# Attention with a pair sum added by an accumulating transfer, and two sum rounds on TensorE instead of three

## The chip, the cores and the metric

The kernel runs on one core of one Trainium2 chip. The metric is the time of one execution on the device in microseconds (us). The kernel before takes 3239.81 us, the median of three runs (3238.47 to 3241.17). Engine names: PE is TensorE's matmul, PEld its weight load, DVE is VectorE, ACT is ScalarE, POOL is GpSimd, SP is SyncE, whose queue issues all transfers of the kernel before.

## What is computed

One transformer block in float32, for 8 batches of 1024 tokens with 512 features: x plus attention of the normalised x, then that plus a gated feed-forward part. The change touches the attention alone. Its core is this, with 16 heads of 32 features, so that a group of four heads fills 128 partitions:

```python
attn = jnp.einsum('bhqd,bhkd->bhqk', query, key) / scale
attn = jax.nn.softmax(attn, axis=-1)
out = jnp.einsum('bhqk,bhkd->bhqd', attn, value)
```

The kernel takes the exponentials first, multiplies them with the values, and divides by their sum over the keys later. The change is in how this sum over the keys is built.

## The kernel before, in words

Four stages follow each other: fold_block folds the weights, project_block makes queries, keys and values, attend_block does the attention, mix_block the output projection and the feed-forward part. attend_block goes through 32 groups (a batch and four heads, step(i, r, n)). A group has 8 units, four for each half of the queries (qc = 0 and 1, 512 queries each). I number halves through as h = 2n + qc. A unit is two tiles of 128 keys for each of four heads: 8 score tiles of 128x512.

For each unit TensorE computes 8 score tiles (L804) into three PSUM buffers, and between them 8 products of the next group (L264) from which VectorE takes row maxima (L280); at two places in a group (units 4 and 0) a transpose of the collected maxima (L259) stands between them and VectorE turns it into the row that SP then writes into the next group's queries (L277, L290). ScalarE takes the exponential of each score tile (L892) into one of three buffers probs, each a whole unit. After the scores of unit u TensorE multiplies the probabilities of unit u - 1 with the values (pv, L817). GpSimd adds the two key tiles of a unit (L911): one 128x2048 addition, the pair sum pairs[w], w = 0 to 3 for the unit in its half. After pair sum 1 it adds pair sum 0 onto it (L915). I call the sum of two pair sums a quad.

The sum over the keys is finished by TensorE in sums(n, qc): rounds of four matmuls with a matrix of ones (L828), each over one buffer of pairs, accumulated in PSUM; a float32 matmul shows as two records. There are three rounds, over pairs[1] (the quad), pairs[2] and pairs[3]. They stand after the scores and pv of unit 4 for the first half and of unit 0 of the next group for the second. ScalarE copies the result out (take_l, L876) before the exponentials of the unit that follows, just after the output of the half (take_o, L869), and SP stores both (L749, L754).

The order on each engine is written out by hand, with counting semaphores between engines. GpSimd waits before it writes pairs[w]: for w = 0 until its own quad of the half before is done, for the others until TensorE's round over the buffer in the half before is done. ScalarE waits, before it writes a probs buffer, for pv and for the pair sum of the unit three before it. L_AT says at which score tile the PSUM buffer of the sums is taken from the three. SP's queue, in order: the 10 loads for the group after next (L242 to L247), stores of the last half, the row of maxima, stores of the first half, the row of maxima of the second.

Of the kernel before, what the change touches and what calls it, by code (L numbers as in the profile page):

```python
# [21 lines left out]
ALU = mybir.AluOpType  # L22
# [20 lines left out]
def is_first(c):  # L43

    return type(c) is int and c == 0
# [161 lines left out]
NQ = S // CH  # L207
# [466 lines left out]
def attend_block(nc, sem, held, t, att, scratch, o_d, l_d):  # L674
# [5 lines left out]
    ROUNDS = KT // KB  # L680
    UNITS = NQ * ROUNDS
    UT = KB * HG
    TILES = UNITS * UT
    SR = 3
    PR = 3
    ADDED = [1, 2, 4, 5]
    ADDS = ROUNDS + 1
    SUMMED = [1, 2, 3]
    SUMS = len(SUMMED)
    RUN = TILES + NQ  # L690
    L_AT = UT
    HALF_RUN = ROUNDS * UT + 1
    assert RUN % SR == 0 and R3 * UNITS % PR == 0

    def is_last(n):
        return type(n) is int and n == NG - 1

    def place(e):

        return e + (e >= L_AT) + (e >= L_AT + ROUNDS * UT)  # L700

    def l_place(n, qc):

        return RUN if is_last(n) and qc == NQ - 1 else L_AT + (qc + 1) * HALF_RUN

    def taken(n, v):

        if is_first(n):
            return v + (v < L_AT)
        return n * RUN + v  # L710

    with ExitStack() as ctx:
        def sb(name, shape, dt=F32):
            return ctx.enter_context(nc.sbuf_tensor(name, shape, dt))
# [6 lines left out]
        pairs = sb("pairs", [P, ROUNDS, HG, CH])  # L721
# [8 lines left out]
        exped = sem("exped")  # L730
        pv_done = sem("pv_done")
        pair_done = sem("pair_done")
        sum_done = sem("sum_done")
        o_out = sem("o_out")
        o_stored = [sem(f"o_stored{q}") for q in range(NQ)]
# [3 lines left out]
        def rounds(step):  # L739

            for n in range(NG):
                step(n // R3, n % R3, n)
# [49 lines left out]
        @block.tensor  # L792
        def _(pe):
            def scores(n, r, u, x):
                qc, w = divmod(u, ROUNDS)
                a, kt = x % HG, w * KB + x // HG
                v = place(u * UT + x)
                if u == 0 and x == 0 and type(n) is int and n == 1:
                    pe.wait_ge(rows_set, 16 * (R3 - 1))
                if w == 0 and x == 0:  # L800
                    pe.wait_ge(m_stacked[qc], 16 * (n + 1))
                if v >= SR or not is_first(n):
                    pe.wait_ge(exped, taken(n, v - SR))
                nc.tensor.matmul(ps_s[v % SR][:, :], ks[r][:, a, kt * P:(kt + 1) * P],  # L804
                                 qs[r][:, qc, a, :], start=True, stop=True).then_inc(scored, 1)

            def pv(n, i, r, u):
                qc, w = divmod(u, ROUNDS)
                if u == 0:
                    pe.wait_ge(v_loaded[r], 16 * (i + 1))  # L810
                if w == 0 and not (is_first(n) and qc == 0):
                    pe.wait_ge(o_out, n * NQ + qc)
                pe.wait_ge(exped, taken(n, place(u * UT + UT - 1)))
                for k in range(KB):
                    kt = w * KB + k
                    for a in range(HG):
                        m = nc.tensor.matmul(ps_o[a * HD:(a + 1) * HD, :], vt[r][:, kt, a * HD:(a + 1) * HD],  # L817
                                             probs[:, (r * UNITS + u) % PR, k, a, :], start=kt == 0, stop=kt == KT - 1)
                m.then_inc(pv_done, 1)

            def sums(n, qc):

                v = l_place(n, qc)
                pe.wait_ge(exped, taken(n, v - SR))
                for k, w in enumerate(SUMMED):
                    pe.wait_ge(pair_done, (n * NQ + qc) * ADDS + k + 3)
                    for a in range(HG):
                        m = nc.tensor.matmul(ps_s[v % SR][a * HD:(a + 1) * HD, :], ones[:, :], pairs[:, w, a, :],  # L828
                                             start=k == 0, stop=k == SUMS - 1)
                    m.then_inc(sum_done, 1)  # L830

            def step(i, r, n):


                r1 = (r + 1) % R3
                i1 = i + 1 if r1 == 0 else i
                todo = [] if is_last(n) else list(range(STEPS))
                spread = SPREAD_FIRST if is_first(n) else SPREAD

                def maxima(count):  # L840
                    for _ in range(count if todo else 0):
                        max_product(nc, pe, att, ps_m, t["ident"], n + 1, r1, i1 + 1, todo.pop(0))

                for u in range(UNITS):
                    for x in range(UT):
                        maxima(spread[u][x])
                        scores(n, r, u, x)
                    if u >= 1:
                        pv(n, i, r, u - 1)
                        if u == ROUNDS:  # L850
                            sums(n, 0)
                    elif not is_first(n):
                        pv(n - 1, i if r else i - 1, (r - 1) % R3, UNITS - 1)
                        sums(n - 1, 1)
                    maxima(spread[u][UT])
                if is_last(n):
                    pv(n, i, r, UNITS - 1)
                    sums(n, 1)

            pe.wait_ge(att["ones_done"], 1)  # L860
            rounds(step)

        @block.scalar
        def _(act):
            def take_o(n, qc):
                act.wait_ge(pv_done, n * UNITS + (qc + 1) * ROUNDS)
                if not is_first(n):
                    act.wait_ge(o_stored[qc], 16 * n)
                nc.scalar.copy(o_sb[:, qc, :], ps_o[:, :]).then_inc(o_out, 1)  # L869

            def take_l(n, qc):
                v = l_place(n, qc)
                act.wait_ge(sum_done, (n * NQ + qc + 1) * SUMS)
                if not is_first(n):
                    act.wait_ge(l_stored[qc], 16 * n)
                nc.scalar.copy(l_sb[:, qc, :], ps_s[v % SR][:, :]).then_inc(exped, 1)  # L876

            def step(i, r, n):
                for u in range(UNITS):
                    if u == ROUNDS + 1:  # L880
                        take_o(n, 0)
                        take_l(n, 0)
                    if u == 1 and not is_first(n):
                        take_o(n - 1, 1)
                        take_l(n - 1, 1)
                    if u >= PR or not is_first(n):
                        act.wait_ge(pv_done, n * UNITS + u - PR + 1)
                        qc, w = divmod(u - PR, ROUNDS)
                        act.wait_ge(pair_done, (n * NQ + qc) * ADDS + ADDED[w])
                    for x in range(UT):  # L890
                        act.wait_ge(scored, n * TILES + u * UT + x + 1)
                        nc.scalar.activation(probs[:, (r * UNITS + u) % PR, x // HG, x % HG, :], ps_s[place(u * UT + x) % SR][:, :],  # L892
                                             ACT.Exp, scale=SCALE).then_inc(exped, 1)
                if is_last(n):
                    take_o(n, 1)
                    take_l(n, 1)

            rounds(step)

        @block.gpsimd  # L900
        def _(pool):
            def step(i, r, n):
                for u in range(UNITS):
                    qc, w = divmod(u, ROUNDS)
                    if not (is_first(n) and qc == 0):
                        if w == 0:
                            pool.wait_ge(pair_done, (n * NQ + qc) * ADDS)
                        else:
                            pool.wait_ge(sum_done, (n * NQ + qc - 1) * SUMS + w)
                    pool.wait_ge(exped, taken(n, place(u * UT + UT - 1)))  # L910
                    nc.gpsimd.tensor_tensor(pairs[:, w, :, :], probs[:, (r * UNITS + u) % PR, 0, :, :], probs[:, (r * UNITS + u) % PR, 1, :, :],  # L911
                                            ALU.add).then_inc(pair_done, 1)
                    if w == 1:
                        pool.wait_ge(pair_done, (n * NQ + qc) * ADDS + 2)
                        nc.gpsimd.tensor_tensor(pairs[:, 1, :, :], pairs[:, 0, :, :], pairs[:, 1, :, :],  # L915
                                                ALU.add).then_inc(pair_done, 1)

            rounds(step)
# [590 lines left out]
```

## Time and profile before

| | |
|---|---|
| median of three runs | 3239.81 us |
| profiled execution, its own time | 3239.41 us |
| its span | 3237.6 us |
| granted TensorE clock, mean | 0.981 |
| busy share of the span: PE, DVE, ACT, POOL | 96%, 68%, 46%, 63% |
| attention, from its first to its last sum round (L828) | 730.6 to 2412.0 us in the span |

The span is what the records cover; 1.8 us lie around it. The attention stage fills about half of it and repeats itself every group. The trace gives for each record the start and duration, and for idle time in front of a record what ended it. Matmuls overlap in their records: the start of the next one tells more than the duration.

### The profile page before, as it was taken

The page shows a single profiled execution, that of the slowest core. Times are in us where ns is not written, and L with a number is a line of the kernel's source. Part 1 is how long each engine was busy: PE and PEld are TensorE (multiplying, and loading weights), DVE is VectorE, ACT ScalarE, POOL GpSimd, SP SyncE. Part 2 cuts the span into 40 slices and gives each one's busy share as a digit, 9 for nine tenths or more (in the row PEclk, how much of TensorE's full clock was granted, in tenths as well). Part 3 has the DMA queues.
Part 4 walks back from the last instruction along what each step waited for, and adds up shares of the span by engine and source line. Part 5 has one row for each costly group of instructions (what it writes and reads, how often), then busy time and mean ns, then how long its engine had stood idle before and what let it go on. Part 6 is the DMA issues. An engine that isn't in the chain of part 4 may idle for free. (4 is left out here: it accounts for less than half of the span.)

```text
span 3237.6 us, 43860 instructions
## 1 busy us (share of the span) xinstructions
PE 3097.1 (96%) x16020; PEld 2049.8 (63%) x16020; DVE 2201.2 (68%) x3337; ACT 1487.9 (46%) x2714; POOL 2034.4 (63%) x654
## 2 busy tenths in 40 slices
PE   7999999989999999999999999999975999999998
PEld 4888888855555555555555555555524778777876
DVE  3555445567777777777777777777718777887784
ACT  1222122226666666666666666666652232233232
POOL 0111112127888888888888888888874566666663
PEclk8999999989999999999999999999987999999999
DMA  3454544652424242424242423333115133233221
GB/s 102 157 188 162 175 167 164 188 144 56 102 57 102 57 102 57 102 57 102 61 100 63 96 68 90 74 85 78 35 49 147 53 105 104 61 95 104 83 73 40
DMA packets 179855, 315.79 MB, mean 98 GB/s; under 512 B 16081, under 2 KB 52081, under 8 KB 179697
## 3 DMA queue, kind: packets, MB, share of 16 engines
q1 hardware_dynamic: 179696, 313.70, 35.1%
q8 instruction: 97, 1.59, 0.2%
q14 instruction: 62, 0.50, 0.1%
HBM read 194.59 MB, written 118.49 MB: 97 GB/s over the span
## 5 line engine op out<-in xcount | busy, mean ns | idle before, releaser
L280 DVE TENSOR_REDUCE part_max<-ps_m 128x1 f32<-128x512 f32 x1984 | 1211.8, 681 | 415.3 <-PE ps_m L264 415.3
L911 POOL TENSOR_TENSOR pairs<-probs 128x2048 f32<-128x2048 f32 x256 | 1169.3, 4577 | 307.3 <-ACT probs L892 302.2
L892 ACT ACTIVATE probs<-ps_s 128x512 f32<-128x512 f32 x2048 | 1036.8, 624 | 429.4 <-PE ps_s L804 357.9
L264 PE MATMUL ps_m<-k_stack,q_stack 96*128 96x512 f32 x1984 | 817.2, 413 | 40.3 <-DVE neg_max L277 34.2
L804 PE MATMUL ps_s<-q_stack,k_stack 97*128 97x512 f32 x2048 | 818.3, 402 | 6.2 <-PEq L313 4.1
L264 PEld LDWEIGHTS ps_m<-k_stack,q_stack 96*128 96x128 f32 x1984 | 377.1, 190 | 307.8 <-DVE part_max L280 136.0
L817 PE MATMUL ps_o<-probs,v_tiles 128*32 128x512 f32 x4096 | 494.8, 601 | 0.0
L804 PEld LDWEIGHTS ps_s<-q_stack,k_stack 97*128 97x128 f32 x2048 | 387.9, 190 | 136.7 <-ACT probs L892 21.7
L548 POOL TENSOR_TENSOR y_cos<-y_rot,cos 64x512 f32<-64x512 f32 x16 | 20.5, 1283 | 475.6 <-DVE y_swap L644 475.6
L915 POOL TENSOR_TENSOR pairs<-pairs 128x2048 f32<-128x2048 f32 x64 | 293.1, 4579 | 5.0
L817 PEld LDWEIGHTS ps_o<-probs,v_tiles 128*32 128x32 f32 x4096 | 107.3, 109 | 233.6 <-issue 177.0
L1274 POOL TENSOR_TENSOR gate<-gate,xs 128x512 f32<-128x512 f32 x64 | 115.2, 1802 | 131.3 <-DVE diff L1340 113.8
L828 PE MATMUL ps_s<-pairs,ones 128*32 128x512 f32 x1536 | 176.7, 592 | 1.3 <-POOL pairs L911 1.3
L1194 ACT ACTIVATE relu<-mix_p 128x512 f32<-128x512 f32 x64 | 38.3, 598 | 240.9 <-PE mix_p L1092 186.0
L1358 DVE TENSOR_TENSOR ka_lo<-relu,ka_hi 128x512 fp32r<-128x512 f32 x64 | 112.8, 1762 | 47.8 <-ACT ka_hi L1188 45.5
L1090 PE MATMUL mix_p<-mix_w_o_hi,o_hi 128*128 128x512 f32 x256 | 103.5, 404 | 42.3 <-DVE o_lo L1384 26.8
L1243 POOL TENSOR_TENSOR xs<-mix_x_in,bo 128x512 f32<-128x512 f32 x64 | 115.0, 1801 | 25.9 <-DMA mix_x_in<-in_x 21.5
L828 PEld LDWEIGHTS ps_s<-pairs,ones 128*32 128x32 f32 x1536 | 49.8, 110 | 116.6 <-issue 113.1
L621 DVE TENSOR_TENSOR st_v<-ps_p,bv 128x512 f32<-128x512 f32 x64 | 44.2, 690 | 98.1 <-PE ps_p L450 98.1
L1090 PE MATMUL mix_p<-mix_w_v_hi,ka_hi 128*128 128x512 f32 x256 | 102.6, 401 | 8.4 <-DVE ka_lo L1358 8.3
L1332 DVE SCALAR_TENSOR_TENSOR mixed<-diff,mu_k,xT 128x512 f32<-128x512 f32 x64 | 109.3, 1747 | 0.6
L1261 POOL TENSOR_TENSOR relu<-relu 128x512 f32<-128x512 f32 x64 | 68.8, 1085 | 64.1 <-ACT relu L1194 64.1
(178 smaller groups left out, 4748.8 us busy)
## 6 DMA issues: line engine op xcount, KB each, us to landing
q_stack<-q_hi_scratch SPq DMA_DIRECT2D x128, 256.0 KB, 5.8
k_stack<-k_hi_scratch SPq DMA_DIRECT2D x64, 512.0 KB, 10.3
x_in<-in_x SPq DMA_DIRECT2D x16, 1024.0 KB, 5.5
q_hi_scratch<-st_hi SPq DMA_DIRECT2D x64, 256.0 KB, 2.3
q_lo_scratch<-st_lo SPq DMA_DIRECT2D x64, 256.0 KB, 2.5
k_hi_scratch<-st_hi SPq DMA_DIRECT2D x64, 256.0 KB, 2.4
k_lo_scratch<-st_lo SPq DMA_DIRECT2D x64, 256.0 KB, 2.7
v_scratch<-st_v SPq DMA_DIRECT2D x64, 256.0 KB, 2.3
```

Of the source, the lines that this page charges most:

```text
L264: nc.tensor.matmul(bank[:, :], att["q"][r][0:ROWS, half, h, q * P:(q + 1) * P], att["k"][r][0:ROWS, h, kc * CH:(kc + 1) * CH], start=True, ...
L280: nc.vector.reduce_max(part_max[:, half, j, kc:kc + 1], bank[:, :], AX).then_inc(att["m_read"], 1)
L804: nc.tensor.matmul(ps_s[v % SR][:, :], ks[r][:, a, kt * P:(kt + 1) * P], qs[r][:, qc, a, :], start=True, stop=True).then_inc(scored, 1)
L817: m = nc.tensor.matmul(ps_o[a * HD:(a + 1) * HD, :], vt[r][:, kt, a * HD:(a + 1) * HD], probs[:, (r * UNITS + u) % PR, k, a, :], start=kt ...
L828: m = nc.tensor.matmul(ps_s[v % SR][a * HD:(a + 1) * HD, :], ones[:, :], pairs[:, w, a, :], start=k == 0, stop=k == SUMS - 1)
L892: nc.scalar.activation(probs[:, (r * UNITS + u) % PR, x // HG, x % HG, :], ps_s[place(u * UT + x) % SR][:, :], ACT.Exp, scale=SCALE).then_ ...
L911: nc.gpsimd.tensor_tensor(pairs[:, w, :, :], probs[:, (r * UNITS + u) % PR, 0, :, :], probs[:, (r * UNITS + u) % PR, 1, :, :], ALU.add).th ...
L915: nc.gpsimd.tensor_tensor(pairs[:, 1, :, :], pairs[:, 0, :, :], pairs[:, 1, :, :], ALU.add).then_inc(pair_done, 1)
L1090: nc.tensor.matmul(out, stat_hi(f), mov_hi(f), start=f == 0, stop=False)
L1243: nc.gpsimd.tensor_tensor(xs[par][:, s, :], x_in[:, s, :], bo[:, :], ALU.add).then_inc(xb_done, 1)
L1274: nc.gpsimd.tensor_tensor(gate[:, s, :], gate[:, s, :], xs[par][:, s, :], ALU.add).then_inc(out_done, 1)
L1358: nc.vector.tensor_tensor(ka_lo[:, g, :], relu[:, g % RELU, :], ka_hi[:, g, :], ALU.subtract).then_inc(kal_done, 1)
```

## The change

GpSimd's quad of the first two pair sums goes. In its place GpSimd issues a transfer from pairs[0] to pairs[1] that accumulates (accum_op add), 1 MB of float32, with a semaphore of its own, joined. GpSimd makes a quad of pair sums 2 and 3 instead, after pair sum 3. TensorE has two rounds, over pairs[1] and pairs[3], the first behind joined, the second behind the quad. They stand one unit later (after unit 5, and after unit 1 of the next group), and so does ScalarE's take_l; take_o stays. GpSimd's waits follow: pairs[0] is free when the transfer of the half before has landed, pairs[1] after round 1 of the half before, pairs[2] after its quad, pairs[3] after round 2.

```diff
-    ADDED = [1, 2, 4, 5]
     ADDS = ROUNDS + 1
-    SUMMED = [1, 2, 3]
+    SUMMED = [1, 3]
     SUMS = len(SUMMED)
     RUN = TILES + NQ
-    L_AT = UT
+    L_AT = 2 * UT
...
                 for k, w in enumerate(SUMMED):
-                    pe.wait_ge(pair_done, (n * NQ + qc) * ADDS + k + 3)
+                    if k == 0:
+                        pe.wait_ge(joined, 16 * (n * NQ + qc + 1))
+                    else:
+                        pe.wait_ge(pair_done, (n * NQ + qc + 1) * ADDS)
...
                     if u >= 1:
                         pv(n, i, r, u - 1)
-                        if u == ROUNDS:
+                        if u == ROUNDS + 1:
                             sums(n, 0)
+                        if u == 1 and not is_first(n):
+                            sums(n - 1, 1)
                     elif not is_first(n):
                         pv(n - 1, i if r else i - 1, (r - 1) % R3, UNITS - 1)
-                        sums(n - 1, 1)
...
                     if u == ROUNDS + 1:
                         take_o(n, 0)
+                    if u == ROUNDS + 2:
                         take_l(n, 0)
                     if u == 1 and not is_first(n):
                         take_o(n - 1, 1)
+                    if u == 2 and not is_first(n):
                         take_l(n - 1, 1)
...
-                        act.wait_ge(pair_done, (n * NQ + qc) * ADDS + ADDED[w])
+                        act.wait_ge(pair_done, (n * NQ + qc) * ADDS + w + 1)
...
                         if w == 0:
-                            pool.wait_ge(pair_done, (n * NQ + qc) * ADDS)
+                            pool.wait_ge(joined, 16 * h)
+                        elif w == 1:
+                            pool.wait_ge(sum_done, (h - 1) * SUMS + 1)
+                        elif w == 2:
+                            pool.wait_ge(pair_done, h * ADDS)
                         else:
-                            pool.wait_ge(sum_done, (n * NQ + qc - 1) * SUMS + w)
+                            pool.wait_ge(sum_done, h * SUMS)
...
                     if w == 1:
-                        pool.wait_ge(pair_done, (n * NQ + qc) * ADDS + 2)
-                        nc.gpsimd.tensor_tensor(pairs[:, 1, :, :], pairs[:, 0, :, :], pairs[:, 1, :, :],
+                        pool.wait_ge(pair_done, h * ADDS + 2)
+                        nc.gpsimd.dma_start(pairs[:, 1, :, :], pairs[:, 0, :, :], accum_op=ALU.add).then_inc(joined, 16)
+                    if w == 3:
+                        pool.wait_ge(pair_done, h * ADDS + 4)
+                        nc.gpsimd.tensor_tensor(pairs[:, 3, :, :], pairs[:, 2, :, :], pairs[:, 3, :, :],
                                                 ALU.add).then_inc(pair_done, 1)
```

## Rows read from the trace of the kernel before

**Rows 1.** The page, part 1: span, and busy time, share and instructions by engine.

```profile
span 3237.6 us, 43860 instructions
PE 3097.1 (96%) x16020; PEld 2049.8 (63%) x16020; DVE 2201.2 (68%) x3337; ACT 1487.9 (46%) x2714; POOL 2034.4 (63%) x654
```

**Rows 2.** Busy time by engine in 1400 us of attention, clock, DMA share, GB/s.

```profile
core 0: us, PE busy (x) PEld busy (x) DVE busy (x) ACT busy (x) POOL busy (x), PEclk, DMA share, GB/s
800.00:2200.00 1400.00, 1370.62 (x8028) 750.48 (x8027) 1049.44 (x1789) 910.38 (x1787) 1200.08 (x264) 1.00 0.34 79
```

**Rows 3.** Groups by line, 800 to 2300 us: busy us, mean ns, idle before, releasers.

```profile
L280 DVE TENSOR_REDUCE part_max<-ps_m 128x1 f32<-128x512 f32 x1803 | 1101.0, 681 | 360.6 <-PE ps_m L264 360.6
...
L264 PE MATMUL ps_m<-k_stack,q_stack 96*128 96x512 f32 x1803 | 740.9, 411 | 31.2 <-DVE neg_max L277 31.2
...
L828 PE MATMUL ps_s<-pairs,ones 128*32 128x512 f32 x1344 | 154.5, 592 | 0.0
```

**Rows 4.** Timeline of PE over one group: start us, duration us, record, count.

```profile
1503.48 0.50 PE L264 MATMUL ps_m<-k_stack,q_stack 96*128 96x512 f32 x1 [0.37 <-DVE neg_max L277]
...
1507.42 1.93 PE L817 MATMUL ps_o<-probs,v_tiles 128*32 128x512 f32 x16
1509.16 2.76 PE L828 MATMUL ps_s<-pairs,ones 128*32 128x512 f32 x24
1511.85 0.50 PE L264 MATMUL ps_m<-k_stack,q_stack 96*128 96x512 f32 x1
...
1515.80 1.93 PE L817 MATMUL ps_o<-probs,v_tiles 128*32 128x512 f32 x16
1517.65 0.50 PE L264 MATMUL ps_m<-k_stack,q_stack 96*128 96x512 f32 x1
...
1529.26 0.50 PE L264 MATMUL ps_m<-k_stack,q_stack 96*128 96x512 f32 x1
...
1536.08 2.76 PE L828 MATMUL ps_s<-pairs,ones 128*32 128x512 f32 x24
1538.77 0.50 PE L264 MATMUL ps_m<-k_stack,q_stack 96*128 96x512 f32 x1
...
1550.35 0.50 PE L264 MATMUL ps_m<-k_stack,q_stack 96*128 96x512 f32 x1
...
1562.49 2.76 PE L828 MATMUL ps_s<-pairs,ones 128*32 128x512 f32 x24
```

**Rows 5.** Timeline of POOL in the same group.

```profile
1516.87 4.59 POOL L911 TENSOR_TENSOR pairs<-probs 128x2048 f32<-128x2048 f32 x1 [3.43 <-ACT probs L892]
1521.53 4.59 POOL L915 TENSOR_TENSOR pairs<-pairs 128x2048 f32<-128x2048 f32 x1
1526.09 13.76 POOL L911 TENSOR_TENSOR pairs<-probs 128x2048 f32<-128x2048 f32 x3
1543.79 4.59 POOL L911 TENSOR_TENSOR pairs<-probs 128x2048 f32<-128x2048 f32 x1 [3.93 <-ACT probs L892]
```

**Rows 6.** Timeline of SP's queue: two of its issues in the same group.

```profile
1514.67 0.54 SPq L754 DMA_DIRECT2D l_scratch<-l_sb  x1
1531.36 0.53 SPq L290 DMA_DIRECT2D q_stack<-neg_max  x1
```

**Rows 7.** Timeline of ACT: the exponentials of one unit.

```profile
1518.50 4.03 ACT L892 ACTIVATE probs<-ps_s 128x512 f32<-128x512 f32 x8 [1.78 <-PE ps_s L804]
```

**Rows 8.** DMA issues: count, KB each, median us from issue to landing.

```profile
x_in<-in_x SPq DMA_DIRECT2D x16, 1024.0 KB, 5.5
...
v_tiles<-v_scratch SPq DMA_DIRECT2D x32, 512.0 KB, 13.9
```

**Rows 9.** Busy time by engine in two stretches of the group, with the DMA share.

```profile
1524.00:1530.00 6.00, 6.00 (x34) 3.52 (x33) 5.25 (x10) 4.03 (x8) 6.00 (x2) 1.00 0.59 167
1530.00:1539.00 9.00, 8.25 (x56) 3.75 (x56) 4.96 (x9) 4.81 (x10) 8.91 (x3) 1.00 0.09 31
```

**Rows 10.** Timeline of ACT at the end of the attention.

```profile
2400.53 4.03 ACT L892 ACTIVATE probs<-ps_s 128x512 f32<-128x512 f32 x8 [1.48 <-PE ps_s L804]
...
2413.05 0.58 ACT L876 COPY l_sb<-ps_s 128x512 f32<-128x512 f32 x1 [3.53 <-PE ps_s L828]
```

More of the change, by code:

```diff
@@ L732, in attend_block @@
         pair_done = sem("pair_done")
+        joined = sem("joined")
         sum_done = sem("sum_done")
@@ L904, in step @@
                     qc, w = divmod(u, ROUNDS)
+                    h = n * NQ + qc
                     if not (is_first(n) and qc == 0):
                         if w == 0:
-                            pool.wait_ge(pair_done, (n * NQ + qc) * ADDS)
+                            pool.wait_ge(joined, 16 * h)
[3 more added lines that the diff above has]
+                            pool.wait_ge(pair_done, h * ADDS)
                         else:
-                            pool.wait_ge(sum_done, (n * NQ + qc - 1) * SUMS + w)
+                            pool.wait_ge(sum_done, h * SUMS)
                     pool.wait_ge(exped, taken(n, place(u * UT + UT - 1)))
```

## The prediction

> **What bounds the kernel now.** I read the page's first part, then the busy times of the attention by stretches, then the groups by line, then one group instruction by instruction. The page names TensorE: 3097.1 of 3237.6 us [rows 1]. That alone is a mean over four stages; in 1400 us of attention it is 1370.62 us, with POOL at 1200.08, DVE at 1049.44 and ACT at 910.38, at full granted clock [rows 2]. The reader should see that TensorE has 2% left and GpSimd 14%. By line, TensorE's only wait of weight is 31.2 us in 1500 for the negated maxima, which the change leaves alone; its sum rounds wait for nothing [rows 3]. The largest waits are those of the others on TensorE: DVE's maxima sat 360.6 us for its products [rows 3]. So in this stage time taken from TensorE's queue is time taken from the kernel, as long as no other engine becomes the slower one.
>
> The group from 1503.48 shows the rhythm. Sum rounds begin at 1509.16, 1536.08 and 1562.49 [rows 4]: halves of 26.92 and 26.41 us, a group of 53.33 us, a mean half of 26.67. GpSimd does five additions of 4.59 us in each half, and waits once, 3.43 or 3.93 us, for the exponentials of the second unit [rows 5]. These numbers decide the case.
>
> **The removed round.** From a pv's start to the next product it is 4.43 us with three rounds behind it (1507.42 to 1511.85) and 1.85 us without (1515.80 to 1517.65) [rows 4]: 2.58 us for three rounds, 0.86 for one. Nothing hides it: it lies on the full engine. 64 rounds go; of these 62 stand before the last group's end phase or inside the steady part, 62 x 0.86 = 53.3 us. The other two I count in the end phase below.
>
> **The moved rounds, and what moves with them.** A unit without sums takes TensorE 5.80 us (1511.85 to 1517.65), units 2 and 3 together 11.61, unit 4 without its sums 9.51 - 2.58 = 6.93, units 5 and 6 11.58, and unit 7 what is left of 53.33, 6.46; unit 0 without its sums 8.37 - 2.58 = 5.79 [rows 4]. With two rounds in units 1 and 5 (1.72 us each) the new group is 5.79 + 7.52 + 11.61 + 6.93 + 7.50 + 5.80 + 6.46 = 51.61 us. I count time in it from the start of unit 0: unit 1 starts at 5.8, unit 2 at 13.3, unit 4 at 24.9, unit 5 at 31.9, unit 6 at 39.4, unit 7 at 45.2. ACT's copy of the sums moves behind eight more exponentials; it then waits for TensorE as it does now, and the score that reuses its PSUM buffer is again the third behind it, so I cost it at nothing. Its store moves past nothing in SP's order: SP issues it (0.54 us, at 1514.67) one unit later, and the next thing in its queue is the row of maxima at 1531.36, some 17 us behind [rows 6]; one unit takes 6 to 8 of them. Were that cover gone, a late row would hold the next group's first score, but that comes 20 us after the row.
>
> **GpSimd.** It keeps five additions: the first quad goes, the second comes. With its waits on itself (from the end of 1516.87's addition to 1521.53 is 0.07 us [rows 5]) that is 5 x 4.58 + 2 x 0.07 = 23.04 us for a half, plus d, the time for which issuing the transfer holds it. Behind the issue in its queue stand pair sum 2, pair sum 3, the quad and pair sum 0; whoever waits for these waits for d too. Exponentials of a unit end 4.9 us after its start (1518.50 + 4.03 against 1517.65) [rows 4, 7]. The new wait that bites is pair sum 1's, for round 1 of the half before. That round ends 6.7 us into unit 1 or 5 (3.94 to the pv, 1.74 to the rounds, 0.86, and 0.2 of drain), at 12.5 and 38.6. So pair sum 1 runs 12.6 to 17.2, the issue ends at 17.2 + d, pair sum 2 waits for exponentials until 18.2, pair sum 3 runs 24.0 to 28.6, the quad to 33.2, the next pair sum 0 to 37.8, and pair sum 1 waits until 38.65. From pair sum 1 to pair sum 1 it is 26.05 us and 25.56 us: d up to 2.5 us costs nothing, up to 2.8 almost nothing. The quad is there at 33.2 and round 2 comes at 38.4. ACT needs pair sum 1 for unit 4's exponentials at 25: 8 us early.
>
> What d is, no row shows; this kernel issues nothing from GpSimd. The near end is SP's issue of one transfer, 0.54 us [rows 6]. The far end is that GpSimd is held for the whole transfer: 5.5 us, a plain load of 1 MB [rows 8]. I take 1.0, near the issue row, since issuing is all that is asked of it, and twice it as a margin.
>
> **The transfer.** It starts at 18.2 and round 1 of its half comes at 31.9 + 5.7 = 37.6, so it has 19.4 us; in the other half (44.2 to 63.1) 18.9. Its length L has no row either. A plain 1 MB takes 5.5 us [rows 8]; this one reads two operands, so I take 11. The far end is to queue behind the loads of a group, as v_tiles does with 13.9 us [rows 8], and then run its own 11: 24.9. But the loads thin out already at 1524 to 1530 (DMA share 0.59) and are over by 1530 (0.09) [rows 9], and in this clock the first half's transfer starts at 1521.7. So L is covered by the two units of delay; if the cover is gone, TensorE waits in each half. Loads that it delays are due in the next group, 25 us later.
>
> **The end.** In the last group there are no maxima and GpSimd sets the end. Now: exponentials of the last unit end at 2400.53 + 4.03 = 2404.56, and the sums are copied at 2413.05 [rows 10]. New, on the same clock: exponentials at 2404.56 - 0.86 = 2403.7, pair sum 3 to 2408.3, quad to 2412.9, one round and drain 1.1: 2414.0. That is 1.0 us later.
>
> **The sum.** -53.3 + 1.0 = -52.3 us, against the profiled execution's 3239.41: 3187.1 us. Its median stands 0.4 us higher, which is nothing here. Bounds of this case: by busy time a round is 154.5 us / 168 = 0.92 [rows 3], which gives 64 x 0.92 = 58.9 and 3181; with d = 2.5 the end is 1.5 us later and some of the slack is gone: 3192.
>
> **Rivals.** (1) **GpSimd is held longer and becomes the bound.** Then a half is 23.04 + d. Between 2.8 and 3.6 us the gain shrinks to nothing (1a). From d = 3.6 the kernel is slower (1b): at 5.5 a half is 28.54, +1.87 us over 62 halves = +116, and +8 in the last group, where halves are shorter now: 3363 us. For it: GpSimd has only 14% left [rows 2] and no row shows its issue. Against: an issue row would have to grow sevenfold. The Trainium skill, "DMA: Bandwidth & Descriptors", section "Anatomy of one DMA", gives 2.0 us plus bytes over 436 GB/s for a transfer issued by GpSimd, 4.4 us for this one, most of it not on GpSimd; if GpSimd were held for all of it, an estimate by that page is +0.77 x 62 = +48 and about 3290 us.
>
> (2) **The transfer lands too late.** Pair sum 1, issue, transfer and round 1 form a ring, since the next pair sum 1 waits for round 1: 4.65 + 1.0 + L + 1.0 = L + 6.7 us. It decides from L = 19.4. At 24.9 in the halves that meet the loads, the half is 31.6 instead of 26.05, the group 57.2 against 53.33: +3.8 x 31 = +118, 3357 us. For it: 13.9 us to landing under load [rows 8]. Against: idle DMA engines from 1530 on [rows 9].
>
> (3) **It does not do what it says:** TensorE's saved 0.86 us comes back as a wait on DVE, whose maxima lose the pause of the sums in units 0 and 4. Time: about 3240. Against: DVE works 1049.44 of 1400 [rows 2] and is itself waiting for TensorE.
>
> **How the numbers follow.** Forecast 0.62 (3181 to 3192). Rival 1a 0.12 (3192 to 3240). Rival 1b 0.13 (3240 to 3363). Rival 2 0.09 (from 3240 up). Rival 3 0.04. Faster is 0.62 and 0.10 of 1a, 0.72; same, within 0.2% or 6.5 us (about what a measurement of this kernel can tell from no change), the rest of 1a and most of rival 3, 0.05; slower 0.23. The range goes from 3180 over the forecast and 1a (0.74) into 1b as far as it must to leave out no more than 0.2: four tenths of the way from 3240 to 3363, 3290. The forecast's own range is 3180 to 3193.
>
> **What the profile of the changed kernel would show.** L828 with 1024 records instead of 1536; sum starts 25.6 to 26.05 us apart; POOL still with five additions of 4.58 us a half and a short gap after pair sum 1; PE busy still 97% or more in the attention. I am wrong if PE's rounds or weight loads show idle time released by POOL or a DMA in each half, if the gap behind pair sum 1 on POOL is over 2.8 us, or if the additions on POOL themselves grow.

## Result, and the profile after

The changed kernel takes 3190.78 us (median of four runs, 3185.31 to 3193.76) against 3239.14 us of the kernel before beside it (four runs): ratio 0.985, 95% interval 0.9835 to 0.9864, 48 us less. The profiled execution is the fastest of the four, 3185.31 us, which is 54.1 us less than the profiled one of before (3239.41). The forecast was 3187.

The page of the changed kernel, part 1:

```profile
span 3183.5 us, 42900 instructions
PE 3038.1 (95%) x15508; PEld 2030.9 (64%) x15508; DVE 2193.7 (69%) x3337; ACT 1488.2 (47%) x2714; POOL 2096.1 (66%) x718
```

Against [rows 1], TensorE has 512 records fewer, the 64 rounds, and 59 us less busy time; GpSimd has 64 instructions more, the issues. Now the 1400 us of attention of [rows 2], and two of its groups by line (800 to 2250 us; busy, mean ns, idle before):

```profile
800.00:2200.00 1400.00, 1369.67 (x7872) 761.38 (x7869) 1083.86 (x1847) 939.91 (x1845) 1292.74 (x326) 1.00 0.55 124
```

```profile
L264 PE MATMUL ps_m<-k_stack,q_stack 96*128 96x512 f32 x1800 | 739.0, 411 | 31.1 <-DVE neg_max L277 31.1
...
L831 PE MATMUL ps_s<-pairs,ones 128*32 128x512 f32 x896 | 106.4, 592 | 0.0
```

The reader should see that TensorE is as full as before, 1369.67 us of 1400 against 1370.62, and its rounds (L831, formerly L828) still wait for nothing: it does the same attention, with one round fewer in each half, in less time, while GpSimd rose from 1200.08 to 1292.74. The time went where a round was taken out of a full queue. The timeline of TensorE shows the two rounds behind the pv of units 1 and 5:

```profile
1503.85 0.50 PE L264 MATMUL ps_m<-k_stack,q_stack 96*128 96x512 f32 x1 [0.74 <-DVE neg_max L277]
...
1512.65 1.92 PE L817 MATMUL ps_o<-probs,v_tiles 128*32 128x512 f32 x16
1514.40 1.90 PE L831 MATMUL ps_s<-pairs,ones 128*32 128x512 f32 x16
...
1539.95 1.90 PE L831 MATMUL ps_s<-pairs,ones 128*32 128x512 f32 x16
...
1555.42 0.50 PE L264 MATMUL ps_m<-k_stack,q_stack 96*128 96x512 f32 x1 [0.74 <-DVE neg_max L277]
```

Group to group is 1555.42 - 1503.85 = 51.57 us, where [rows 4] had 53.33. On GpSimd a half looks so, where [rows 5] had a wait of 3.43 or 3.93 us:

```profile
1515.55 4.61 POOL L922 TENSOR_TENSOR pairs<-probs 128x2048 f32<-128x2048 f32 x1 [0.75 <-PE ps_s L831]
1520.45 0.88 POOL L926 DMA_DIRECT2D pairs<-pairs  x1 [0.30 <-POOL pairs L922]
1521.26 4.71 POOL L922 TENSOR_TENSOR pairs<-probs 128x2048 f32<-128x2048 f32 x1
1527.04 4.58 POOL L922 TENSOR_TENSOR pairs<-probs 128x2048 f32<-128x2048 f32 x1 [1.07 <-ACT probs L898]
1531.70 4.58 POOL L929 TENSOR_TENSOR pairs<-pairs 128x2048 f32<-128x2048 f32 x1
1536.25 4.58 POOL L922 TENSOR_TENSOR pairs<-probs 128x2048 f32<-128x2048 f32 x1
1541.10 4.61 POOL L922 TENSOR_TENSOR pairs<-probs 128x2048 f32<-128x2048 f32 x1 [0.27 <-PE ps_s L831]
```

Pair sum 1, the issue, pair sums 2 and 3, the quad, the next pair sum 0, the next pair sum 1: two short waits in each half, one for exponentials (1.07 us), one for round 1 (0.75 or 0.27). The transfer has a row of its own among the DMA issues (count, KB, median us to landing), and the last load of a group lands later than before, 16.1 us after its issue instead of 13.9 [rows 8]:

```profile
pairs<-pairs POOLq DMA_DIRECT2D x64, 1024.0 KB, 8.0
...
v_tiles<-v_scratch SPq DMA_DIRECT2D x32, 512.0 KB, 16.1
```

The 8.0 is a median over two kinds of transfer. Between 800 and 2200 us, those in the halves without loads land in 7.0 us (the one issued at 1520.45, for example), those in the halves whose transfers run beside the loads (SP issues these from 1482.9 to 1487.1) in 11.6 to 13.3, median 12.5 (the one issued at 1494.43: 12.7).

The end of the attention, on ScalarE, against [rows 10]:

```profile
2344.12 4.03 ACT L898 ACTIVATE probs<-ps_s 128x512 f32<-128x512 f32 x8 [1.49 <-PE ps_s L804]
2350.87 0.58 ACT L873 COPY o_sb<-ps_o 128x512 f32<-128x512 f32 x1 [2.73 <-PE ps_o L817]
2359.72 0.58 ACT L880 COPY l_sb<-ps_s 128x512 f32<-128x512 f32 x1 [8.26 <-PE ps_s L831]
```

and the round that it waits for, on TensorE:

```profile
2357.72 1.94 PE L831 MATMUL ps_s<-pairs,ones 128*32 128x512 f32 x8 [5.83 <-POOL pairs L929]
```

The last copy starts 53.3 us earlier (2413.05 to 2359.72). GpSimd's first addition started 0.9 us earlier already (694.90 to 694.0), so 52.4 us come from the attention. The other 1.7 us between the two profiled executions lie in stages that the change does not touch.

### The profile page after: what moved, and what is told of

The parts are those of the page before. It is cut to its first block and busy times, and to the rows that moved or that the text cites. A ratio compares the mean times of both kernels' runs of the same rounds, so it can differ in the third digit from the quotient of the medians.

```text
span 3183.5 us, 42900 instructions
## 1 busy us (share of the span) xinstructions
PE 3038.1 (95%) x15508; PEld 2030.9 (64%) x15508; DVE 2193.7 (69%) x3337; ACT 1488.2 (47%) x2714; POOL 2096.1 (66%) x718
## 3 DMA queue, kind: packets, MB, share of 16 engines
q0 software_dynamic: 9216, 67.11, 10.3%
## 5 line engine op out<-in xcount | busy, mean ns | idle before, releaser
L922 POOL TENSOR_TENSOR pairs<-probs 128x2048 f32<-128x2048 f32 x256 | 1181.9, 4619 | 170.4 <-ACT probs L898 135.6
L1372 DVE TENSOR_TENSOR ka_lo<-relu,ka_hi 128x512 fp32r<-128x512 f32 x64 | 104.3, 1629 | 47.9 <-ACT ka_hi L1202 45.6
L831 PE MATMUL ps_s<-pairs,ones 128*32 128x512 f32 x1024 | 122.7, 596 | 5.8 <-POOL pairs L929 5.8
L880 ACT COPY l_sb<-ps_s 128x512 f32<-128x512 f32 x64 | 37.6, 587 | 183.7 <-PE ps_s L831 183.7
```

The source lines that it names most:

```text
L1372: nc.vector.tensor_tensor(ka_lo[:, g, :], relu[:, g % RELU, :], ka_hi[:, g, :], ALU.subtract).then_inc(kal_done, 1)
```

## The experiments

Each edit is made to the changed kernel unless said. Times are medians, "before" is the kernel before, measured beside it on the same chip.

**Is it the later place?** In the kernel before, only the place of the three rounds and of the copy is moved, as in the change:

```diff
-    L_AT = UT
+    L_AT = 2 * UT
...
-                        if u == ROUNDS:
+                        if u == ROUNDS + 1:
                             sums(n, 0)
```

> The kernel before with its three sum rounds and the copy of the sums one unit later, nothing else. Theory (TensorE's queue sets the time, a removed round is the gain): the queue is as long as before, so 3239 us, within 5. Rival (the later place is the gain, because the rounds no longer come just behind the last pair sum): 3225 us or less. Second rival (moving the copy behind more exponentials costs something): 3246 or more.

Measured: 3242.78 us over ten runs, before 3242.41; ratio 0.9998, 0.9989 to 1.0008. The place alone is worth nothing.

**Is it GpSimd's relief, or does the transfer cost something?** The second quad is taken out and round 2 put back:

```diff
-    SUMMED = [1, 3]
+    SUMMED = [1, 2, 3]
...
-                    if w == 3:
-                        pool.wait_ge(pair_done, h * ADDS + 4)
-                        nc.gpsimd.tensor_tensor(pairs[:, 3, :, :], pairs[:, 2, :, :], pairs[:, 3, :, :],
-                                                ALU.add).then_inc(pair_done, 1)
```

> The changed kernel without the quad of pair sums 2 and 3: the transfer adds pair sum 0 onto 1, and TensorE has three rounds again, over pairs 1, 2 and 3. GpSimd has four additions and one issue a half. Theory (TensorE's rounds): as before, 3239 us, within 5, although GpSimd works 4 us less in each half. Rival (GpSimd held the kernel back before): 3225 or less. Rival (1 MB more on the DMA engines each half slows loads or rows of maxima): 3246 or more.

Measured: 3239.45 us, before 3242.41; ratio 0.9988, 0.9978 to 0.9997. That is at most 7 us of the 48, with GpSimd at 1010.21 us of 1400 in place of 1200.08 [rows 2] and TensorE where it was:

```profile
800.00:2200.00 1400.00, 1370.57 (x8020) 749.73 (x8019) 1047.58 (x1787) 908.61 (x1784) 1010.21 (x264) 1.00 0.53 119
```

With three rounds a half the rest of the change gains next to nothing, and 1 MB more a half on the DMA engines (their share rises from 0.34 to 0.53) costs nothing either.

**Is the transfer needed?** GpSimd makes both quads itself:

```diff
-                        nc.gpsimd.dma_start(pairs[:, 1, :, :], pairs[:, 0, :, :], accum_op=ALU.add).then_inc(joined, 16)
+                        nc.gpsimd.tensor_tensor(pairs[:, 1, :, :], pairs[:, 0, :, :], pairs[:, 1, :, :],
+                                                ALU.add).then_inc(pair_done, 1)
```

> The changed kernel with the transfer replaced by GpSimd's own addition: six additions a half, two rounds, sums in the later place. Theory (GpSimd becomes the slower engine without the transfer): a half is 6 x 4.58 + 0.2 = 27.7 us instead of 26.67 before, +64 us, and some 6 in the last group, 3309 us. Rival (GpSimd has room enough, the transfer is not needed): 3187 us.

Measured: 3299.6 us, ratio 1.0174 (1.0157 to 1.0191). Two of its quads on GpSimd, a half apart:

```profile
1514.79 4.57 POOL L925 TENSOR_TENSOR pairs<-pairs 128x2048 f32<-128x2048 f32 x1
...
1542.42 4.58 POOL L925 TENSOR_TENSOR pairs<-pairs 128x2048 f32<-128x2048 f32 x1
```

27.63 us, as worked out (27.7), and GpSimd without a pause; the time expected was 3309. The same two rounds that gain 48 us behind the transfer lose 57 behind an addition.

**Is the later place needed with the quad?** Sums, copy and PSUM place go back behind units 4 and 0 (L_AT = UT, sums and take_l where they were).

> The changed kernel with the sums, the copy and its PSUM place where they stood before (after units 4 and 0). Theory (the quad on GpSimd ends 9.2 us after the last exponentials of its half, and round 2 would come at 32.6 and 6.5 us in the group where the quad ends at 33.4 and 7.7): TensorE waits about 2.0 us in each group, 31 x 2.0 = 62 us, which takes the whole gain back: 3249 us, 3235 to 3255. Rival (the delay is not needed, the transfer of 8 us has landed in time): 3187 us.

Measured: 3259.65 us, before 3242.41; ratio 1.0052 (1.0035 to 1.0069). TensorE's rounds in one group:

```profile
1512.54 1.04 PE L831 MATMUL ps_s<-pairs,ones 128*32 128x512 f32 x8
1514.70 1.07 PE L831 MATMUL ps_s<-pairs,ones 128*32 128x512 f32 x8 [1.11 <-POOL pairs L926]
...
1541.58 1.06 PE L831 MATMUL ps_s<-pairs,ones 128*32 128x512 f32 x8 [0.63 <-POOL pairs L926]
...
1568.47 1.07 PE L831 MATMUL ps_s<-pairs,ones 128*32 128x512 f32 x8 [1.11 <-POOL pairs L926]
```

The wait is for the quad (L926), not for the transfer: round 1 starts on time, round 2 waits 1.11 and 0.63 us in the records. That makes 1.74 us a group, but from start to start the group is 1568.47 - 1514.70 = 53.77 us, 2.2 more than the 51.57 of the changed kernel, and 31 x 2.2 = 68. By the ratios it stands 1.0052 - 0.9853 = 2.0% above the changed kernel, some 65 us. I had said 2.0 us a group and at most 3255, so it came out 5 us beyond that. So the delay is for GpSimd's quad, and without it the change is slower than the kernel before.

**How wide is the room on GpSimd?** The changed kernel again as a control, and three kernels with one more addition behind each issue (here 1024 columns; 256 and 2048 in the others):

```diff
+                        nc.gpsimd.tensor_tensor(spare[:, :], pairs[:, 0, :, :].rearrange("p a t -> p (a t)")[:, 0:1024],
+                                                pairs[:, 0, :, :].rearrange("p a t -> p (a t)")[:, 0:1024], ALU.add)
```

> The changed kernel once more, for its own spread. The profiled execution was 3185.3 us and the others 3190 to 3194. Theory (the scatter is in the granted clock): median 3187 to 3192, single runs follow the clock. Rival (the profiled one was an outlier): all at 3190 or over.

> The changed kernel with one more addition on GpSimd behind each issue, 128x256, its result unused: 0.6 to 0.9 us. GpSimd now works 24.3 us of a half of 25.8, so 1.5 us are free. Theory: no change, 3190 us within 5. Rival (GpSimd already sets the half): +0.6 x 64 = 38 us or more.

> The same with 128x1024 elements, t = 2.2 to 3.6 us. Theory (room of 1.5 us a half, then GpSimd sets the pace): 3190 + 62 x (t - 1.5), so 3233 us at t = 2.2. Rival (longer room, since TensorE's two units of delay buffer it): 3190.

> The changed kernel with an extra addition of 128x2048 on GpSimd behind each issue, result unused, about 4.4 us (1024 elements took 2.20 us, of which 1.85 lengthened the half). By the 1024 run GpSimd alone needs 25.93 - 1.85 = 24.08 us a half, so this half is 24.08 + 4.05 = 28.1 us instead of 25.8: +2.35 x 62 = +146 us, 3338 us, 3320 to 3360; that is also the price of rival 1b of the prediction (GpSimd held for over 5 us). Rival (GpSimd's surplus is taken up by the delay of the sums): 3240 or less.

Measured: control 3192.79 us (before 3240.39; ratio 0.9853, 0.9837 to 0.987); 256 columns 3192.39 (0.9851, 0.9834 to 0.9867); 1024 columns 3201.13 (0.9877, 0.986 to 0.9893); 2048 columns 3304.08 (before 3238.94; 1.0202, 1.0184 to 1.0219). With 1024 columns GpSimd has no pause left but the 0.30 us before each issue. Two issues, a half apart, and the extra addition with what follows it:

```profile
1499.15 0.89 POOL L927 DMA_DIRECT2D pairs<-pairs  x1 [0.30 <-POOL pairs L923]
1499.77 2.20 POOL L928 TENSOR_TENSOR spare<-pairs 128x1024 f32<-128x1024 f32 x1
1501.62 9.40 POOL L923 TENSOR_TENSOR pairs<-probs 128x2048 f32<-128x2048 f32 x2
...
1525.09 0.89 POOL L927 DMA_DIRECT2D pairs<-pairs  x1 [0.30 <-POOL pairs L923]
```

The half is 25.94 us. Pair sum 2 starts 2.47 us after the issue (1499.15 to 1501.62), in the changed kernel 0.81 (1520.45 to 1521.26): the extra work takes 1.66 us of the queue, not its record of 2.20, since its start moves up to 0.62 us behind the issue's. So GpSimd needs 25.94 - 1.66 = 24.28 us by itself, where the forecast had 23.04 + 1.0. The changed kernel's own half says the same: 51.57 / 2 = 25.79, less GpSimd's waits of 1.07 and 0.51 (the mean of 0.75 and 0.27), is 24.21, and the room 1.6 us. The 1024 columns cost 0.15 x 62 = 9 us; I had expected 43, with 1.5 us of room, which was about right, and 2.2 us of work, which was not. With 2048 columns:

```profile
1515.85 0.89 POOL L927 DMA_DIRECT2D pairs<-pairs  x1 [0.30 <-POOL pairs L923]
1516.47 3.90 POOL L928 TENSOR_TENSOR spare<-pairs 128x2048 f32<-128x2048 f32 x1
1520.03 9.44 POOL L923 TENSOR_TENSOR pairs<-probs 128x2048 f32<-128x2048 f32 x2
...
1543.43 0.89 POOL L927 DMA_DIRECT2D pairs<-pairs  x1 [0.30 <-POOL pairs L923]
```

Half 27.58, extra 4.18 - 0.81 = 3.37, GpSimd alone 24.21; (27.58 - 25.79) x 62 = 111 us, measured 3304.08 - 3192.79 = 111. The time expected was 3338, 3320 to 3360, because I took the record for 4.4 us and it was 3.90; the rule it was to test, that what GpSimd's work exceeds the half by is paid 62 times, holds.

The control's profiled execution was 3191.24 us. Between its first and last sum round it has 4 us more than the profiled one of the result (738.6 to 2363.8 against 737.4 to 2358.6); in its last group the granted clock is 0.83 in 2310 to 2320, in the other it is 1.00 until 2350, and the stretch from the pv of unit 1 to the last half's round 1 is 1.7 us longer. The steady groups have the rest: 51.65 us against 51.57, means of 26, which is 2.4 us over 31; why is not known. So the scatter of some 9 us sits partly in the last group, where TensorE has gaps, and 3185.31 was the good end of it.

**What does the accumulation cost the transfer?** A plain copy into a spare buffer, and three rounds over pairs 0, 1 and 3:

```diff
-                        nc.gpsimd.dma_start(pairs[:, 1, :, :], pairs[:, 0, :, :], accum_op=ALU.add).then_inc(joined, 16)
+                        nc.gpsimd.dma_start(spare[:, :, :], pairs[:, 0, :, :]).then_inc(joined, 16)
```

> The transfer of the changed kernel as a plain copy into a spare buffer that nobody reads; TensorE has three rounds, over pairs 0, 1 and 3, the first two behind the copy. It measures what the accumulation adds to transfer and issue. Theory (two reads for one write make the accumulating transfer longer): to landing 5 to 6 us instead of 8.0, issue about 0.9 as before; time 3239 us within 6. Rival (issue and length do not depend on it): 8.0 us.

Measured: one run, 3246.01 us beside 3242.34. The transfer's own line and its landing, plain, and then accumulating in the changed kernel:

```profile
L928 POOL DMA_DIRECT2D spare<-pairs x64: 577/577/761, 703.4 to 2401.5; - x64
...
DMA to landing us min/median/max: 4.4/4.7/11.8
```

```profile
L926 POOL DMA_DIRECT2D pairs<-pairs x64: 875/884/1057, 703.3 to 2343.1; - x64
...
DMA to landing us min/median/max: 6.9/8.0/13.3
```

By the medians the same megabyte takes 1.7 times as long to land when it accumulates. Taken apart by halves (800 to 2200 us), it is 7.0 against 4.6 us without loads and 12.5 against 5.8 beside them: a factor of 1.5 alone and 2.2 under load. It is not the number of rounds: the accumulating transfer of the kernel with three rounds lands in 7.0 and 12.4 us. GpSimd's issue is 0.88 instead of 0.58 us; I had expected no difference there. The Trainium skill, "DMA: Bandwidth & Descriptors", section "Anatomy of one DMA", gives 2.0 us plus bytes over 436 GB/s, an estimate of 4.4 us for this size. The plain copy without loads agrees (4.4 at the least, 4.6 in the median); the accumulating one, 6.9 at the least, is beyond it.

**Both quads by transfer.**

```diff
-                        nc.gpsimd.tensor_tensor(pairs[:, 3, :, :], pairs[:, 2, :, :], pairs[:, 3, :, :],
-                                                ALU.add).then_inc(pair_done, 1)
+                        nc.gpsimd.dma_start(pairs[:, 3, :, :], pairs[:, 2, :, :], accum_op=ALU.add).then_inc(joined2, 16)
```

> The changed kernel with both quads by transfer: GpSimd has four additions and two issues a half, TensorE two rounds. Theory (TensorE's queue sets the half): the same in the steady part; at the end of the attention a transfer of 8 us and its issue stand where an addition of 4.6 us stood, +4.5 us: 3195 us, 3189 to 3200. Rival (GpSimd's 94% still costs something in each half): 3180 or less. Rival (two transfers a half collide with the loads): 3210 or more.

Measured: 3198.74 us (ratio 0.9876, 0.986 to 0.9893), the control beside it 3192.79. TensorE's last round waits for the transfer:

```profile
2370.12 1.93 PE L832 MATMUL ps_s<-pairs,ones 128*32 128x512 f32 x8 [7.14 <-DMA pairs<-pairs]
```

In the steady part GpSimd's relief gains nothing: a group takes 51.73 us, against 51.57 in the changed kernel (means of 26). At the end the landing costs: from the end of the last exponentials to the copy of the sums it is 14.3 us instead of 11.6, so 2.8 of the 6 us. For the rest, the granted clock in the last group was 0.81 and 0.68 in 2320 to 2340, where it was 1.00 in the changed kernel; whether that comes with the second transfer one profiled execution cannot tell.

**One round.** The step further, and the only try at a kernel better than both:

```diff
-    SUMMED = [1, 3]
+    SUMMED = [3]
...
+                        pool.wait_ge(joined, 16 * (h + 1))
+                        pool.wait_ge(pair_done, (h + 1) * ADDS)
+                        nc.gpsimd.dma_start(pairs[:, 3, :, :], pairs[:, 1 if h % 2 == 0 else 4, :, :], accum_op=ALU.add).then_inc(joined2, 16)
```

> One round instead of two: behind the quad of pair sums 2 and 3 a second transfer adds the first quad onto it, TensorE has one round, again one unit later, and pair sum 1 has two buffers in turn. If TensorE alone set the half, 53 us less than the changed kernel and some 8 more at the end: 3145 us. Theory: TensorE's half falls to 24.9 us and GpSimd's work rises to 5 x 4.6 + 2 x 1.1 + 0.2 = 25.4, so GpSimd sets the half: 0.4 x 62 = 25 less, 8 more at the end, 3172 us.

Measured: 3396.1 us, ratio 1.0473 (1.0456 to 1.0491). Neither sum had the wait in it that now decides. GpSimd issues the second transfer at 1519.65, SP the loads from 1517.01, and the round comes at 1528.5:

```profile
1534.73 1.94 PE L829 MATMUL ps_s<-pairs,ones 128*32 128x512 f32 x8 [6.22 <-DMA pairs<-pairs]
```

```profile
1522.00:1528.00 6.00, 6.00 (x40) 3.37 (x32) 5.08 (x9) 4.03 (x8) 6.00 (x2) 1.00 1.09 237
1528.00:1534.00 6.00, 0.51 (x8) 0.00 (x0) 0.03 (x1) 0.00 (x0) 5.70 (x3) 0.83 1.00 245
1534.00:1540.00 6.00, 5.26 (x18) 3.00 (x19) 2.34 (x4) 2.47 (x5) 1.39 (x1) 0.60 1.08 248
```

The columns are stretch, its length, busy PE, PEld, DVE, ACT, POOL, then granted clock, DMA share, GB/s. TensorE stands still, and the clock falls to 0.60 behind it: the lower of its two levels (1.2 instead of 2.4 GHz) for most of these 6 us. The eight records of the round take 1.94 us instead of 1.04. TensorE waits for a transfer 30 times in the run, once a group, 177 us in all: the second transfer lands in 11.6 to 15.7 us in the halves that meet the loads and in 7.0 (median) in the others.

To part the loads from the ring, the loads were issued two units later (wait for pv_done at n * UNITS + 2):

> The one-round kernel with the loads of the group after next issued two units later, so that they no longer meet the second transfer of the second half. Theory (one round is lost to TensorE's wait for that transfer, which landed only after some 14 us beside the loads, and to the clock that fell in the wait): no wait of TensorE beyond 1 us in a half, the second transfer lands in 8 to 10 us in most halves, granted clock back at 0.98, and GpSimd sets the half at about 25.2 us: 3166 us, 3155 to 3190. Rival (the ring of two transfers is too long by itself): 3250 or more.

Measured: 3335.33 us, ratio 1.0298 (1.0281 to 1.0316), 61 less (57 by the ratios), but far from 3166. One half in two still waits:

```profile
1531.72 1.94 PE L829 MATMUL ps_s<-pairs,ones 128*32 128x512 f32 x8 [4.18 <-DMA pairs<-pairs]
```

Its transfer was issued at 1518.78, the round wanted it at 1527.5, 8.8 us later, and it landed after 12.8 us. The next one, issued at 1549.93, landed after 7.0, and its round at 1558.96 did not wait. The median of 8.8 us over all transfers lies between the two kinds. Before the late one the DMA engines were full:

```profile
1513.00:1519.00 6.00, 6.00 (x34) 3.53 (x33) 4.83 (x9) 4.70 (x10) 5.38 (x3) 1.00 1.05 225
1519.00:1525.00 6.00, 6.00 (x34) 3.56 (x34) 5.07 (x9) 4.22 (x10) 6.00 (x3) 1.00 1.05 254
```

The loads, issued until 1510 now, meet the first transfer of this half (issued at 1503.53, 12.2 us to landing), and the second one still lands late. So the edit did not part the loads from the ring, and the theory was not put to the test that it was meant for. The time came out where the rival had it (3250 or more), but the rival's cause, a ring of two transfers that is too long by itself, is not shown either: where no loads run, the ring closes without a wait. What part of the loss the loads, the two transfers and the fallen clock each take stays open. A later place of the round with one more buffer was not tried.

## Why the prediction was right

- **The bound.** "Time taken from TensorE's queue is time taken from the kernel" held: full before and after, and with the round put back the gain is gone (3239.45 against 3242.41).
- **The round.** 62 x 0.86 us. The group fell by 53.33 - 51.57 = 1.76 us, two rounds of 0.88. The term was 0.02 us a round too small.
- **GpSimd.** 24.04 us a half were forecast; 24.21, 24.28 and 24.21 are what the changed kernel and the kernels with 1024 and 2048 columns give. The gap behind pair sum 1 was 1.10 us, forecast d = 1.0, well under the 2.8 that would have mattered.
- **The transfer.** L was taken as 11 us, twice a plain megabyte. It measured 7.0 without loads and 12.5 beside them, at most 13.3, always under the 18.9 that it has, so that the cover held although 11 fits neither kind. The reason given (it reads two operands) fits the direction, 7.0 against 4.6 plain; that it is the reason, no run shows.
- **The end.** Here two errors cancel, and that the sum came out to 0.1 us (-52.3 forecast, -52.4 by the profiled executions) is luck. The last exponentials were to start 53.3 + 0.86 = 54.2 us earlier and started 2400.53 - 2344.12 - 0.9 = 55.5 earlier: 63 rounds of 0.88. From their end to the last copy it was to be 10.3 us (2403.7 to 2414.0) and was 11.6 (2348.15 to 2359.72), 8.5 before. Of these 1.3 us too many, 0.9 are the last round: it was put at 1.1 us with its drain and took 2.0, since its records, behind TensorE's wait of 5.83 us for the quad, take 1.94 us instead of 1.06, at a granted clock of 0.58 (2356 to 2362).
- **Rival 1b**, GpSimd as the bound, was real and near: an extra 3.4 us on GpSimd brought it, 3304 us, slower than before. From the end of pair sum 1 to pair sum 2 it is 0.30 + 4.18 = 4.5 us there, and the forecast's own formula gives a half of 23.04 + 4.5 = 27.54 for this (27.58 measured). Rival 2, the late transfer, does not occur here; the one-round kernels show it, in the halves that meet the loads. Rival 3, a wait on DVE, does not occur: TensorE's wait for maxima is 31.1 us in 1450, 31.2 in 1500 before.
- **What was off** is the median: 48 us were gained in the medians, 52 forecast. The steps compare profiled executions, and the changed kernel's was the fastest of its four, 5.5 us under its median, where the forecast put 0.4 us between the two. In the one control execution that was profiled, 1.7 us of the difference lie in the last group, with the clock, and 2.4 in slightly longer steady groups.

## What to carry to other kernels

When one engine's queue is full, a step taken off it pays its whole length as long as the helper that takes it over keeps a pause in every period: add up the helper's queue, issue times included, and compare it with the new, shorter period, not with the old. The transfer was worth having here for 1.1 us of GpSimd instead of 4.6, and moving the consumer one unit later is what keeps a slower producer free of charge. A second transfer in the same ring, beside the loads, turned a gain of 48 us into a loss of 154. And a median to landing can hide two kinds of transfer: what has to be covered is the slower kind, 12.5 us here and not 8.0.

## What the runs showed of the hardware

- Records on GpSimd overlap around an issue: the addition behind it starts 0.81 us after the start of an issue of 0.88 (the kernels with an extra addition: 0.62), and extra additions with records of 2.20 and 3.90 us there took only 1.66 and 3.37 of the queue. The period is to be taken from start to start, not from durations.
- GpSimd's issue of a 1 MB transfer over 128 partitions takes 0.88 us accumulating and 0.58 plain; from the end of the addition before to the start of the next it is 1.10 us (accumulating).
- A 1 MB transfer inside SBUF, from issue to landing: accumulating 7.0 us without loads and 12.5 beside them, plain 4.6 and 5.8. The loads suffer too: with three rounds in all of them, the last one of a group lands after 15.6 us (median) with an accumulating transfer a half, 14.3 with a plain one, 13.9 with none.
- Around a standstill of TensorE of 6 us the granted clock fell from 1.00 over 0.83 to 0.60, so that a wait cost more than its length: in the one-round kernel the attention ran at a mean clock of 0.93 between 800 and 2200 us. At the end of the changed kernel's attention, behind a wait of 5.83 us, it was 0.58 (2356 to 2362), and a round took 1.94 us instead of 1.06.
